# Scores with the tokens on the partitions, and the quads of the attention pipelined anew, in a gated cross-attention layer with experts

## What is computed

```python
x = x + tanh(g_xattn) * xattn(layernorm(x), ctx, mask)      # x: 2 x 2048 tokens of 512
x = x + tanh(g_ffn) * ffn(layernorm(x))
# xattn: q = xn@Wq.T+bq, k = ctx@Wk.T+bk, v = ctx@Wv.T+bv (77 context rows)
#        softmax(mask(q@k.T/sqrt(512))) @ v @ Wo.T + bo
# ffn:   probs = softmax(xn @ gate_w.T) over 8 experts; each expert takes its 512 best
#        tokens of each batch; gelu(xin @ w1[e]) @ w2[e], times the gate, added at the token
```

## Time and profile before

| what | value |
|---|---|
| median of 3 runs | 1578.08 us (1573.19 to 1578.4) |
| the profiled execution, its own time | 1578.86 us |
| its span | 1577.1 us |
| mean granted TensorE clock | 0.985 |
| PE busy | 1498.4 us, 95% |
| PE weight loads | 1214.6 us, 77% |
| DVE busy | 1023.2 us, 65% |
| ACT busy | 733.6 us, 47% |
| POOL busy | 574.8 us, 36% |

### The profile page before, as it was taken

How to read it: one execution, slowest core, us unless ns; L and a number is a source line. 1 busy time by engine, 2 the same in 40 slices (tenths; PEclk the granted TensorE clock), 3 DMA queues, 4 the chain that set the end, 5 groups by cost and what they waited for, 6 DMA issues and landing times.

```text
span 1577.1 us, 22321 instructions
## 1 busy us (share of the span) xinstructions
PE 1498.4 (95%) x7169; PEld 1214.6 (77%) x7169; DVE 1023.2 (65%) x1729; ACT 733.6 (47%) x1347; POOL 574.8 (36%) x541
## 2 busy tenths in 40 slices
PE   6887688999999999999999999999999999999996
PEld 5654467787788888888888888888888888888885
DVE  2578777557766767575766667667667665766642
ACT  1384233345444544455445454455445444554432
POOL 2266512453453144432443144404432344323311
PEclk9998799999999999999999999999999999999999
DMA  6175522553432443244323424244334423342133
GB/s 227 59 259 191 161 79 64 137 154 89 90 96 80 94 107 100 89 87 102 107 85 83 110 79 127 57 105 90 99 93 87 115 81 107 81 107 81 40 81 67
DMA packets 101401, 163.58 MB, mean 104 GB/s; under 512 B 7411, under 2 KB 45315, under 8 KB 101285
## 3 DMA queue, kind: packets, MB, share of 16 engines
q1 hardware_dynamic: 86885, 128.50, 26.1%
q0 software_dynamic: 14400, 33.56, 11.5%
HBM read 128.48 MB, written 33.55 MB: 103 GB/s over the span
## 4 chain that ended last, share of the span: by engine, by line
PE 85%; DVE 8%; ACT 2%; issue 2%; POOL 1%; DMA 1%; POOLq 0%; SPq 0%; DVEq 0%; ACTq 0%
PE bank L1325 42%; PE bank L1211 33%; PE bank L1185 4%; PE bank L1480 1%; PE bank L572 1%; PE bank L590 1%; DVE w2hl L1170 1%; PE bank L400 1%; DVE count L852 1%; DVE st L817 1%; DVE onehot L1366 1%; DVE atleast L899 1%; ACT xT L641 1%; DVE sc L793 0%; PE bank L1355 0%
## 5 line engine op out<-in xcount | busy, mean ns | idle before, releaser
L1325 PE MATMUL bank<-w2hl,hh 128*128 128x512 f32 x2048 | 637.8, 393 | 0.0
L1211 PE MATMUL bank<-xo,whl 128*128 128x512 f32 x2352 | 545.1, 390 | 4.8 <-DVE mix L1275 2.8
L1211 PEld LDWEIGHTS bank<-xo,whl 128*128 128x128 f32 x2352 | 441.8, 188 | 100.3 <-DVE mix L1275 3.7
L1325 PEld LDWEIGHTS bank<-w2hl,hh 128*128 128x128 f32 x2048 | 381.7, 189 | 76.5
L1325 PE MATMUL bank<-w2hl,hid_low 128*128 128x512 f32 x1024 | 399.8, 390 | 0.0
L1325 PEld LDWEIGHTS bank<-w2hl,hid_low 128*128 128x128 f32 x1024 | 192.8, 188 | 40.4
L1430 POOL DMA_INDIRECT layer_out<-y,slot_row x64 | 102.8, 1606 | 302.1 <-ACT y L1345 287.3
L1170 DVE TENSOR_TENSOR w2hl<-raw,w2hl 128x512 fp32r<-128x512 f32 x226 | 160.5, 731 | 53.0 <-ACT w2hl L1165 44.1
L1139 POOL TENSOR_TENSOR whl<-raw,whl 128x512 fp32r<-128x512 f32 x56 | 81.6, 1456 | 262.1 <-ACT whl L1105 262.1
L1165 ACT ACTIVATE w2hl<-raw 128x512 fp32r<-128x512 f32 x228 | 136.6, 625 | 58.1 <-DMA raw<-in_L_ffn_w 39.4
L1144 POOL TENSOR_TENSOR whl<-wsum,whl 128x512 fp32r<-128x512 f32 x56 | 75.1, 1340 | 183.6 <-ACT whl L1126 183.6
(11 more groups left out here) (224 smaller groups left out, 1771.8 us busy)
## 6 DMA issues: line engine op xcount, KB each, us to landing
raw<-in_L_ffn_w SPq DMA_DIRECT2D x228, 256.0 KB, 2.7
raw<-in_L_ffn_w SPq DMA_DIRECT2D x72, 512.0 KB, 4.8
x_s<-in_x SPq DMA_DIRECT2D x8, 1024.0 KB, 7.0
layer_out<-x SPq DMA_DIRECT2D x8, 1024.0 KB, 8.9
xn_rows<-xn SPq DMA_DIRECT2D x8, 1024.0 KB, 4.8
raw_k<-in_L_xattn_Wk SPq DMA_DIRECT2D x1, 1024.0 KB, 5.1
raw_q<-in_L_xattn_Wq SPq DMA_DIRECT2D x1, 1024.0 KB, 11.2
raw_v<-in_L_xattn_Wv SPq DMA_DIRECT2D x1, 1024.0 KB, 13.4
```

Source lines behind the costliest of these rows:

```text
L1211: last = pe.matmul(bk[:, :], whl[:, p % 2, part, 2 * w + k, :], xo[:, xpart, x, k, :], start=(not adds and k == 0 and part == HIGH and xpa ...
L1325: last = pe.matmul(Y_BANKS[c][:, :], high if hpart == HIGH else low[:, c * P:(c + 1) * P], w2hl[:, f % 4, part, :], start=(s == 0 and hpar ...
```

## The change

- `qkc` gets an 86th column of -1/512, so that the scores' product also gives minus the mean of x, and `vg` a ninth column of ones, so that the product with the exponentials gives their sum. The pass of sums on ACT (L616), its scale (L620) and the accumulator output of the exponential go.
- The scores are made with 128 tokens of `xT` as the stationary operand and the 86 columns of `qkc` moving, a tile at a time (`score`), so they come out with the tokens on the partitions. `sT`, its copy (L661) and its transposes (L602) go.
- DVE subtracts the maximum itself (`softmax_in`, 128x308), and ACT takes one exponential of 128x308 (`exps`).
- The order is new: quad q + 2 is transposed and quad q + 1 is scored beside quad q. The softmax of quad 0 stands behind the second part of the projections. Two banks instead of three take the transposes, and two take the scores. DVE takes a quad from the scores to the statistics before the next one.
- For quads 4 to 7 (`LATE`) `weigh` gives the row sums of x1 as an accumulator output (`x1sum`), DVE makes the mean (`mean_out`), and ACT the squares (`square_x1`); `bn_stats` and `bn_aggr` stay for quads 0 to 3 alone.
- Batch 0's choice starts in quad 4 and has six places in each quad, so pieces 0 to 5 fall in quad 4, 6 to 11 in quad 5, and `hot_dve` and `slots_dve` in quad 6. POOL gathers beside quad 7. The tokens are turned behind the attention.
- POOL splits the first weights (`w1_low_pool`) behind the gather instead of ahead of it, ACT makes their high part behind the last squares, and ACT's `first_tokens_act` comes ahead of the next weights.

The diff, cut to its core (the removed lines of the loops are those printed above):

```diff
+    LEAD, LATE = 3, 4
     SCALE = float(D) ** -0.5
...
+        turns = [("x", q, i) for q in range(2) for i in range(Q)]
+        for q in range(NQ):
+            turns += [("e", q, 0)]
+            turns += [("x", q + 2, i) for i in range(Q) if q + 2 < NQ]
         turn_at = {t: n for n, t in enumerate(turns)}
-        T_BANKS = (2, 3, 4)
+        T_BANKS = (2, 3)
         O_BANKS = (bank[0], bank[1])
-        VG_BANK, SC_BANK, CHOICE_BANK = bank[5], bank[6], bank[7]
-
-
-        CHOOSE_FROM, PLACES = QB + 1, 3
+        SC_BANKS = (bank[6], bank[4])
+        VG_BANK, CHOICE_BANK = bank[5], bank[7]
+
+
+        CHOOSE_FROM, PLACES = QB, 6
...
+        def score(pe, q, i):
+
+            if i == 0:
+                wait(pe, mean_ready, q - 1)
+                wait(pe, sc_ready, q - 1)
+            pe.wait_ge(turn_out, turn_at["x", q, i] + 1)
+            for k in range(KD):
+                last = pe.matmul(SC_BANKS[q % 2][:, i * JM:(i + 1) * JM], xT[:, q % 2, k, i * P:(i + 1) * P],
+                                 qkc[:, k, q // QB, :], start=(k == 0), stop=(k == KD - 1))
+            if i == Q - 1:
+                last.then_inc(scored, 1)
+
...
+        def route(pe, q):
+
+            pe.wait_ge(turn_out, turn_at["e", q, 0] + 1)
+            wait(pe, rinv_ready, q)
+            for i in range(Q):
+                last = pe.matmul(VG_BANK[:, i * EM:(i + 1) * EM], eT[:, q % 2, i * P:(i + 1) * P], vg[:, q // QB, :],
+                                 start=True, stop=True)
+            last.then_inc(routed, 1)
+
+        def weigh_pe(pe, q, i):
+            n = Q * q + i
+            wait(pe, added, n - 1)
+            pe.matmul(O_BANKS[n % 2][:, :], eT[:, q % 2, i * P:(i + 1) * P], vo[:, q // QB, :],
+                      start=True, stop=True).then_inc(weighed, 1)

         def attention_pe(pe, between):
...
-                    pe.wait_ge(x_in[q % 3], 16 * (q // 3 + 1))
+            wait_evacuated(pe, step_at["mean", 0])
+            pe.wait_ge(tails, 2 * B)
+            for i in range(Q):
+                turn_x(pe, 0, i)
+            for i in range(Q):
+                score(pe, 0, i)
+            for i in range(Q):
+                turn_x(pe, 1, i)
+            prep_pe(pe, 1)
+            for q in range(NQ):
+                if q + 1 < NQ:
+                    score(pe, q + 1, 0)
+                    between(q - 1, 5)
+                    score(pe, q + 1, 1)
+                turn_e(pe, q)
+                if q + 1 < NQ:
+                    score(pe, q + 1, 2)
+                    score(pe, q + 1, 3)
+                between(q, 0)
+                if q == 0:
+                    wait_evacuated(pe, len(steps) - 1)
+                route(pe, q)
+                weigh_pe(pe, q, 0)
+                weigh_pe(pe, q, 1)
+                between(q, 1)
+                weigh_pe(pe, q, 2)
+                between(q, 2)
+                weigh_pe(pe, q, 3)
+                for i in range(Q):
+                    if q + 2 < NQ:
+                        turn_x(pe, q + 2, i)
+                    if i == 0:
+                        between(q, 3)
+                    if i == 2:
+                        between(q, 4)
+
...
+            def square_x1(q, i):
+                if i == 0:
+                    act.wait_ge(x1_mean, q - LATE + 1)
+                    wait(act, deviated2, q - 1)
+                    wait(act, x1_squares, q - LATE)
+                ins = act.activation(spare[:, 1, i, :], x1[:, q % 2, i, :], ACT.Square,
+                                     bias=x1mean[:, q % 2, i:i + 1], accum_out=x1var[:, q % 2, i:i + 1])
+                if i == Q - 1:
+                    ins.then_inc(x1_squares, 1)
+
...
+            def exps(q):
+                act.wait_ge(sm_ready, q + 1)
+                if q >= 2:
+                    act.wait_ge(turned, turn_at["e", q - 2, 0] + 1)
+                act.activation(ex[:, q % 2, :, :], sm[:, q % 2, :, :], ACT.Exp).then_inc(exped, 1)
...
+            for q in range(NQ):
+                exps(q)
+                e_out(q)
+                if q == CHOOSE_FROM:
+                    choice_act(act, 0)
+                if q - 1 >= LATE:
                     for i in range(Q):
...
-                q = it - 1
-                if q >= 0:
...
-                                          bias=xmean[:, q % 2, i:i + 1], accum_out=xvar[:, q % 2, i:i + 1])
-                last.then_inc(squares_done, 1)
-
...
+                square_x1(NQ - 1, i)
+            w1_high_act(act, 0, 0, 0)
...
+                    w1_low_pool(pool, 0, 0, 0)
                 if it == 0:
                     first_deviations(1)
                 q = it - 1
                 if q >= 0:
-                    pool.wait_ge(x1_stats, q + 1)
+                    if q < LATE:
+                        pool.wait_ge(x1_stats, q + 1)
+                    else:
+                        pool.wait_ge(x1_squares, q - LATE + 1)
                     if q >= 2:

                         pool.wait_ge(logit_out, q - 1)
@@ -744,84 +769,113 @@
...
+            def softmax_in(q):
+
+                bk = SC_BANKS[q % 2][:, 0:Q * JM].rearrange("p (i j) -> p i j", i=Q)
+                dve.wait_ge(scored, q + 1)
+                dve.wait_ge(normed1, q + 1)
+                dve.wait_ge(mask_ready, q + 1)
+                for i in range(Q):
+                    last = dve.scalar_tensor_tensor(out=sc[:, i, :], in0=bk[:, i, 0:J],
+                                                    scalar=norm1[:, q % 2, 1, i:i + 1],
+                                                    in1=mbias[:, q % 2, i, :], op0=ALU.mult, op1=ALU.add)
+                    own.mark(last) if i < Q - 1 else last.then_inc(sc_ready, 1)
+                dve.wait_ge(dve_own, own.n)
+                dve.wait_ge(sc_ready, q + 1)
+                step(dve.tensor_reduce(smax[:, :], sc[:, :, :], AX.X, ALU.max))
+                wait(dve, exped, q - 1)
+                dve.tensor_tensor(sm[:, q % 2, :, :], sc[:, :, :], smax[:, :].unsqueeze(2).to_broadcast([P, Q, J]),
+                                  ALU.subtract).then_inc(sm_ready, 1)
+
+            def router_in(q):
+                bk = SC_BANKS[q % 2][:, 0:Q * JM].rearrange("p (i j) -> p i j", i=Q)
+                dve.wait_ge(scored, q + 1)
+
+                if q - 3 >= LEAD:
+                    dve.wait_ge(squares_done, q - 2 - LEAD)
...
+            def weights_in(q):
+                bk = VG_BANK[:, 0:Q * EM].rearrange("p (i e) -> p i e", i=Q)
+                dve.wait_ge(routed, q + 1)
+                own.mark(dve.tensor_copy(lgv[:, q % 2, :, :], bk[:, :, 0:E]))
+                dve.reciprocal(rinv[:, q % 2, :], bk[:, :, E]).then_inc(rinv_ready, 1)
+                dve.wait_ge(rinv_ready, q + 1)
+                dve.wait_ge(dve_own, own.n)
+
...
+                                         op0=ALU.mult, op1=ALU.add,
+                                         accum_out=x1sum[:, q % 2, i:i + 1] if q >= LATE else None)\
+                   .then_inc(added, 1)
...
+            def mean_out(q):
+                dve.wait_ge(added, Q * q + Q)
+
+                dve.tensor_scalar(x1mean[:, q % 2, :], x1sum[:, q % 2, :], -1.0 / D, None, ALU.mult)\
+                   .then_inc(x1_mean, 1)
+
+            router_in(0)
+            prep_out(dve, prep_dve, False, 1, own)
+            for q in range(NQ):
+                softmax_in(q)
+                if 1 <= q <= LATE:
+                    logits_out(q - 1)
+                if q == CHOOSE_FROM:
+                    choice_start_dve(dve, own, 0)
+                if q + 1 < NQ:
+                    router_in(q + 1)
+                between(q, 0)
+                weights_in(q)
+                weigh(q, 0)
+                between(q, 1)
+                weigh(q, 1)
+                weigh(q, 2)
+                between(q, 2)
+                weigh(q, 3)
+                if q < LATE:
+                    stats(q, range(Q))
+                    moments(q)
+                else:
+                    mean_out(q)
+                    between(q, 3)
+                    if q > LATE:
+                        logits_out(q - 1)
+                    between(q, 4)
+                    between(q, 5)
+            for c in range(NC):
                 split_tokens_dve(dve, 0, c)
...
-                    pieces = range(at, N_PIECES) if place == 1 else ()
+            def between(q, place):
+                at = (q - CHOOSE_FROM) * PLACES + place
+                if 0 <= at < N_PIECES + 2:
+                    do(at)
...
+                act.wait_ge(squares_done, NQ - LEAD)
+                act.wait_ge(x1_squares, NQ - LATE)
             act.wait_ge(x_turned, c + 1)
...
```

355 lines of the change are left out of this document (130 added, 225 removed).

## The result

The changed kernel takes 1620.3 us (median of 4 runs, 1619.63 to 1624.31) where the kernel before takes 1576.49: a ratio of 1.0289, 95% interval 1.0265 to 1.0313. It is slower, as forecast, but by 43.8 us instead of 13.6, and the range ended at 1606. The profiled execution took 1619.77 us, its span is 1618.0, 40.9 longer than the span of before. One of the twelve executions of `e9_before_scores`, further down, took 8488.68 us and is not in its ratio.

The account below looks back on a forecast made before the run. The prediction took the early part to be a chain through engines, none full, ending at DVE's first count of batch 1. Count 4.4, accumulators 1.2 and clock 8 gave +13.6 us on 1578.1, so 1592 us, range 1572 to 1606.

Parts of the forecast that it names:

- the second of its two added terms, the clock: Lower PE clock in quads 4 to 7: 23.6 us if always low, 0 if never; a third, 8, taken.
- prices of the lower clock: Slower PE steps that DVE waits for: 6.9 us each in quads 4 and 5, 5.3 in quad 6, 4.5 in quad 7.
- 4.4 us forecast for the count's end: Batch 1's first count on DVE ends at 194.2 instead of 189.8, before clock and accumulators are added.
- start: mask step of quad 0: Projections' last DVE copy comes at some 54.2 (53.5 to 56) instead of 56.1; the quads are counted from there.
- pitch at full clock, quads 0 to 3: Mask step to mask step in early quads: 12.4 us (12.1 to 12.8) for 11.7 before, DVE's order closing the chain.
- quads 4 and 5 together: Six pieces of the choice in each quad: 25.6 and 26.3 us, with about 7 us of DVE idle time each.
- last mask step to the count's end: Behind quad 7: squares, weights, tokens, logits at 188.6 to 189.1, then 5.5 us to the count's end at 194.2.
- the clock falls in the early quads too: Rival: half of quads 1 to 3 low, 3 us each, and two thirds of the later: +30, 1608; chance 0.08.
- The score record: PE's score records with 86 columns moving: 0.083 us each, so 1.3 us for the 16 ahead of `route`.
- The accumulators: Accumulator of `weigh` in 16 tiles on DVE: 0 to 3.2 us, 1.2 taken; by the skill's page nearer the upper end.
- tokens that stood between and POOL's work: Some 3.2 us between logits and count's end that would go, leaving 5.5 of the 8.7 before.
- the faster case: Rival: count's round trip cheaper, quads 4 and 5 take 19 us instead of 26: -8 to -10, 1569; chance 0.17.

Follow-up runs that it names:

- e9_before_scores: Kernel before with only the scores' new orientation, tokens on the partitions; `sT`, its copy and its transposes go: ratio 1.0000.
- e1_fill_all: Changed kernel with spare products where PE waits: ahead of exponential transposes, counts, slot product and third token transposes: 1597.66 us, ratio 1.0139.
- e2_fill_early: Changed kernel with 26 spare products ahead of the exponential transposes in quads 0 to 3 alone: 1607.74 us, ratio 1.0193.
- e8_all: `e1_fill_all` with quad 0's softmax put back first, statistics between products, first weights ahead of squares, 20 spare products ahead of each count: 1594.28 us.
- e11_products_first: `e8_all` with the third and fourth weighing products ahead of PE's counts from quad 4 on: 1586.83 us, ratio 1.0069.

## Why the forecast was wrong, point by point

The chain that the prediction named is the one that the trace shows. The step that failed is the second of its two added terms, the clock: it stood at 8 us, with nothing for the early quads, and the runs put it at some 24. The lengths of the quads with all prices of the lower clock added come close: 25.6 + 6.9 = 32.5 for quad 4 (measured 32.4), 26.3 + 6.9 = 33.2 for quad 5 (32.4), 14.6 + 5.3 = 19.9 for quad 6 (19.5). This fit is in part luck. With spare products the three quads take 72.7 us (`e1_fill_all`), for the 66.5 forecast at full clock: 6.2 more. The 84.3 measured are then 11.6 us of clock, where the prices give 19.1. The two errors nearly cancel. (The clock was still 0.88 and 0.90 in two of these quads, so the 11.6 is a lower bound.) From 4.4 us forecast for the count's end (before the two terms added for clock and accumulators) to the 40.0 measured:

| step of the sum | forecast | measured | off by |
|---|---|---|---|
| start: mask step of quad 0 | 54.2 | 53.5 | -0.7 |
| pitch at full clock, quads 0 to 3 | 12.4 | 13.15 | +3.0 |
| low clock in quads 0 to 3 | 0 | 4.5 twice | +9.0 |
| quads 4 and 5 together | 51.9 | 64.8 | +12.9 |
| quad 6 | 14.6 | 19.5 | +4.9 |
| last mask step to the count's end | 23.9 | 30.3 | +6.4 |
| sum | | | +35.5 |

An estimate of the clock's share of these 35.5 us: 8.7 in the early quads (`e2_fill_early`), 11.6 in quads 4 to 6 (`e1_fill_all`) and 3.4 behind quad 7 (`e8_all` to `e11_products_first`), 23.7 in all. The other 12 are lengths at full clock that the forecast had too short: 3.4 in the early quads, 6.2 in quads 4 to 6 and 3.0 behind quad 7, less 0.7 at the start.

**The clock, the term that failed.** I gave it 8 us, a third of 23.6, "since the gaps are short and the clock held at 1.00 through 195 to 200 itself". The step from one window of the kernel before to "a third" had no row behind it, and the other window, with PE at work in 2.93 of 5 us at 0.50, spoke against it. The mean clock was 0.59, 0.62 and 0.65 in quads 4, 5 and 6, and 0.71 in quads 0 and 2: `e1_fill_all` gives back 20.4 us at the count with the clock still low in part, `e2_fill_early` 9.3 for the early quads alone. The rival "the clock falls in the early quads too" had the right mechanism, and 9 us for it. That matches the 8.7 measured, but as a total only: it had 3 us in each of quads 1 to 3, and the trace has 4.5 in quads 0 and 2. It was given a chance of 0.08 and only two thirds of the later price; with the whole 23.6 its sum would have been 38 us, so 1616. What spoke for it stood in the prediction: PE works some 9.5 of 12.4 us there, with one gap of 2.9 us. The trace shows 10.8 of 13.15 us at full clock, and 2.00 of the rest as a wait for the exponential (73.73). The kernel before is fuller at this place and held its clock, in the window of 80 to 90 us:

```profile
80.00:90.00 10.00, 9.14 (x36) 4.75 (x37) 6.11 (x20) 8.56 (x23) 6.73 (x11) 1.00 0.73 250
```

**The score record, mis-sized.** I took 0.083 us. Sixteen records take 1.92 us, less 0.17 of pipeline end: 0.109 each at full clock, and the eight of `route`, with 9 columns moving, 0.99, so 0.10 each. The 16 weight loads beside the score records are busy for 1.86 us (PEld at 74.12), nearly the whole of their time. The 0.065 of the earlier trace rows was the part of a `vg` record that shows behind the 512 columns of a `vo` record. By my reading its weight load was hidden there, and behind 86 or 9 columns it isn't. With 16 records ahead of `route` (+0.42) and 8 in it (+0.3) that is about the 0.75 by which the quad is longer than forecast. The Trainium skill's rule ("TensorE: Matmul & The Clock Gate", *LDWEIGHTS*), 107 ns for 128 columns, is borne out by these 0.109 and 0.10, and I set it aside for a row that measured something else.

**The accumulators, over-sized.** 1.2 us taken, up to 3.2 allowed. The read is 0.08 us (130.03), and in DVE's timeline the next instruction also starts at 130.03. It is two instructions, but the second costs next to nothing, so the term is at the lower end of 0 to 3.2 and not near the upper.

**Quads 4 and 5 at full clock.** `e8_all` shows 26.75 for quad 4, 1.15 over forecast; by the early quads the score and route records make 0.75 of that. Quad 5 takes 29.7 there, 3.4 over, at a clock of 0.94. The waits are those named, and `e11_products_first` shows that 2.8 us of quad 4 came from PE's order alone, counts ahead of products whose banks were free. The prediction had this wait ("`weigh` 3 needs count, then product") and left it at that.

**Behind quad 7.** Two parts. At the logits' end (221.8, t = 22.3 for 18.3 to 18.8) it is 3.5 to 4 late. The low clock would explain it: 4.5 in the forecast's own price, and 3.4 between `e8_all` and `e11_products_first`. From there to the count's end it takes 8.0 us for 8.7 before; I had 5.5, with 3.2 us "tokens that stood between and POOL's work" gone. Only 0.7 went. The two tokens' steps of before (1.27 us on DVE from 181.85) stood beside ACT's exponential, which DVE has to wait for anyway, and POOL's work is still there. DVE's timeline of the kernel after, batch 0's choice first, then batch 1's, and POOL beside that:

```profile
122.92 0.29 DVE L932 TENSOR_TENSOR prob<-pexp,pstat 128x128 f32<-128x128 f32 x1
123.25 0.22 DVE L947 TENSOR_TENSOR cand<-bit_table,found 128x56 int32<-128x56 int32 x1
123.50 1.09 DVE L951 TENSOR_TENSOR atleast<-prob,cand 128x896 bf16<-128x896 f32 x1
...
223.60 1.04 DVE L932 TENSOR_TENSOR prob<-pexp,pstat 128x128 f32<-128x128 f32 x1
224.68 1.18 DVE L947 TENSOR_TENSOR cand<-bit_table,found 128x56 int32<-128x56 int32 x1
225.89 2.08 DVE L951 TENSOR_TENSOR atleast<-prob,cand 128x896 bf16<-128x896 f32 x1
...
223.23 2.55 POOL L1228 TENSOR_TENSOR w2hl<-raw,w2hl 128x512 fp32r<-128x512 f32 x2
225.75 3.36 POOL L1191 TENSOR_TENSOR whl<-raw,whl 128x512 fp32r<-128x512 f32 x2
```

The same three instructions take 1.60 us by themselves and 4.30 beside POOL's splitting of weights. The kernel before already had this price, and the earlier trace rows pass over it:

```profile
184.74 1.18 DVE L895 TENSOR_TENSOR cand<-bit_table,found 128x56 int32<-128x56 int32 x1
```

The Trainium skill ("SBUF — State Buffer", *SBUF: two separate sides*) says that a VectorE instruction with two SBUF inputs and a GpSimd one that reads SBUF take turns on a shared pair of ports; the rows agree. One run moved the two apart by accident: in `e8_all` POOL's splitting ends at 200.85, ahead of batch 1's three steps, and they take 0.29, 0.22 and 1.09 us, as in batch 0. It was no gain, for the three steps of the logits then stood beside POOL and took 3.7 us instead of 0.6. The last of the three, DVE's timeline of `e8_all`:

```profile
202.57 1.09 DVE L972 TENSOR_TENSOR atleast<-prob,cand 128x896 bf16<-128x896 f32 x1
```

**The falsifiers.** Mask steps "12.4 us apart" came as 13.15 and 17.7. Of the experts' part I wrote that over 3 us of difference would mean that something is missed. By the spans it differs by 0.9 (40.0 at the count, 40.9 at the end), but on the way it moved more: the chain of before and after has the same step at

```profile
515.99 0.87 PE bank L1480 x8
```

```profile
553.01 0.87 PE bank L1541 x8
```

so the kernel after had won back 3 us by then, and lost nearly 4 later, most of it in steps of 0.6 to 1.1. In the other profiled executions the part behind the count is between 2.6 us shorter and 2.1 longer than before. Whether the win and the loss here are scatter of one execution or belong to the change stays open.

**The range.** The direction was right, and the faster case failed on the waits above. The range ended too low because the clock was put at a fraction of its price in every case, though its own bounds were 0 and 23.6, and 9 more with the early quads: with these the upper end would have been 1616. The 4 us that are still missing are lengths at full clock; with the lower clock in all four early quads as well it would have been 1625.

## What to carry to other kernels

When a change opens gaps on PE, price every PE step on the path at the lower clock, for the whole stretch, and let the range reach that sum. Here 8.7 of 18 us came true in the early quads and 15 of 23.6 later, and equal waits went both ways, so no row of the kernel before could have told the exact share. A short record's price should be read from a row where its neighbours are as short as they will be in the new place. Where an engine's order is written by hand, put work whose inputs and banks are ready ahead of work that waits; here that was worth 2.8 us in the one quad where the clock was the same, and 7.5 in all, part of which is the clock.

## What the runs showed of the hardware that I had not expected

- The granted clock fell in quads that keep PE at work for 10.8 of 13.15 us at full clock, at one wait of 2.00 us (86.87) and not at the next one like it (73.73). With 26 spare products, 1.61 us of work, put into PE's wait for the exponential, it was 1.00 from 40 to 100 us in `e1_fill_all`. Quads 1 and 3, which had full clock anyway, stayed at 13.15 us: the spare products cost nothing on the path.
- The lower clock nearly doubles short records, whose time is that of their weight loads: 3.55 us for 1.92.
- An fp32 record with 9 columns moving takes about what one with 86 does, 0.10 and 0.109 us.
- The accumulator read takes 0.08 us on DVE and 0.189 on ACT in this kernel.
- A 128x56 instruction with two inputs in SBUF goes from 0.22 to 1.18 us on DVE beside POOL's splitting of weights, and is back at 0.22 in `e8_all`, where POOL is done before it.
